# A GRU with an expert-choice layer: the two bias rows are loaded in runs of 32 numbers with gaps between them

## The reference, cut to what matters

```python
def cell(h, x):                       # 256 steps, one after the other
    gi = x @ W_ih + b_ih              # 512 -> 3 * 512
    gh = h @ W_hh + b_hh
    r, z = sigmoid(i_r + h_r), sigmoid(i_z + h_z)
    n = tanh(i_n + r * h_n)
    h_new = (1.0 - z) * n + z * h
...
S = softmax(hs @ router_w + router_b)          # 4096 tokens x 16 experts
G, idx = top_k(S.T, 256)
y[idx] += G * (hs[idx] @ expert_w + expert_b)
out = x + y
```

## Time and profile before

| what | value |
|---|---|
| median of 3 runs (lowest to highest) | 1097.17 us (1095.88 to 1097.18) |
| the profiled execution | 1096.32 us, span 1094.6 us |
| TensorE (PE) busy | 1081.6 us, 99% of the span |
| VectorE (DVE) busy | 857.2 us, 78% |
| ScalarE (ACT) busy | 411.3 us, 38% |
| chain that ended last | PE 96%, DVE 1%, DMA 1% |
| granted TensorE clock, mean | 0.998 |

### The profile page before, as it was taken

How to read it: one execution, slowest core, us unless ns; L and a number is a source line. 1 busy time by engine, 2 the same in 40 slices (tenths; PEclk the granted TensorE clock), 3 DMA queues, 4 the chain that set the end, 5 groups by cost and what they waited for, 6 DMA issues and landing times.

```text
span 1094.6 us, 60966 instructions
## 1 busy us (share of the span) xinstructions
PE 1081.6 (99%) x26752; PEld 892.5 (82%) x26752; DVE 857.2 (78%) x4601; ACT 411.3 (38%) x1658; POOL 15.5 (1%) x42
## 2 busy tenths in 40 slices
PE   7999999999999999999999999999999999999998
PEld 5788888888888888888888888888888888888852
DVE  5788777877777877787777778778788777777897
ACT  1333333434333434333333333333333333333561
POOL 5000000000000000000000000000000000000000
PEclk9999999999999999999999999999999999999999
DMA  7311000000000000000000000000000000000369
GB/s 255 90 22 23 13 13 13 6 11 13 13 13 13 14 13 6 11 13 13 14 13 14 13 5 12 13 13 13 13 13 12 6 12 14 3 3 4 100 175 308
DMA packets 80448, 36.78 MB, mean 34 GB/s; under 512 B 70052, under 2 KB 70308, under 8 KB 80183
## 3 DMA queue, kind: packets, MB, share of 16 engines
q1 hardware_dynamic: 77840, 28.79, 10.8%
q10 hardware_dynamic: 2342, 4.11, 1.2%
HBM read 24.49 MB, written 8.39 MB: 30 GB/s over the span
## 4 chain that ended last, share of the span: by engine, by line
PE 96%; DVE 1%; DMA 1%; SPq 0%; ACT 0%; issue 0%; DVEq 0%
PE gates L819 60%; PE gates L756 26%; PE ffn_ps L883 3%; PE gates L937 3%; DMA whh<-in_L_cond_W_hh 1%; PE gates L915 1%; PE ffn_ps L937 1%; PE log_ps L972 1%; PE gates L949 0%; DVE wih L1417 0%; SPq L376 0%; PE ffn_ps L915 0%; DVE u L1186 0%; SPq L379 0%; DVE wih L1507 0%
## 5 line engine op out<-in xcount | busy, mean ns | idle before, releaser
L819 PE MATMUL gates<-whh,tok 128*16 128x192 f32 x16384 | 713.9, 326 | 3.5 <-DVE tok L1211 1.9
L819 PEld LDWEIGHTS gates<-whh,tok 128*16 128x16 f32 x16384 | 562.5, 123 | 104.5 <-DVE tok L1211 3.3
L518 ACT ACTIVATE th<-gates 128x128 f32<-128x128 f32 x512 | 139.8, 273 | 341.7 <-PE gates L819 341.5
L1186 DVE SCALAR_TENSOR_TENSOR u<-th,gates 128x64 f32<-128x64 f32 x512 | 113.5, 222 | 167.0 <-ACT th L518 166.7
L523 ACT ACTIVATE n_t<-v 128x64 f32<-128x64 f32 x512 | 131.5, 257 | 277.9 <-DVE v L1190 277.9
L756 PE MATMUL gates<-wih,xS 128*32 128x192 f32 x3024 | 146.3, 326 | 0.0
L1202 DVE STREAM_TRANSPOSE nT<-n_t 128x64 f32<-128x64 f32 x512 | 123.7, 242 | 0.0
L1193 DVE STREAM_TRANSPOSE zT<-th 128x64 f32<-128x64 f32 x512 | 122.0, 238 | 0.0
L1190 DVE SCALAR_TENSOR_TENSOR v<-u,gates 128x64 f32<-128x64 f32 x512 | 113.1, 221 | 8.8
L756 PEld LDWEIGHTS gates<-wih,xS 128*32 128x32 f32 x3024 | 100.1, 110 | 21.0
L1211 DVE SCALAR_TENSOR_TENSOR tok<-new_n,z_h 128x32 f32<-128x32 f32 x512 | 110.1, 215 | 8.7
(11 more groups left out here) (202 smaller groups left out, 622.2 us busy)
## 6 DMA issues: line engine op xcount, KB each, us to landing
x_in<-in_x SPq DMA_DIRECT2D x248, 32.0 KB, 2.2
out<-tok SPq DMA_DIRECT2D x15, 256.0 KB, 4.7
xs<-in_x SPq DMA_DIRECT2D x14, 256.0 KB, 3.7
out<-tok ACTq DMA_DIRECT2D x14, 256.0 KB, 4.6
wih<-in_L_cond_W_ih SPq DMA_DIRECT2D x4, 768.0 KB, 7.1
whh<-in_L_cond_W_hh SPq DMA_DIRECT2D x4, 768.0 KB, 13.7
whh<-in_x SPq DMA_DIRECT2D x12, 256.0 KB, 3.6
we<-in_L_ffn_expert_w SPq DMA_DIRECT2D x4, 256.0 KB, 2.8
```

The source lines that it names most:

```text
L518: nc.scalar.activation(th[a][:, :, :].rearrange("p g c -> p (g c)"), gates[t // S % PAIRS][a][:, R_:HN], ACT.Tanh, scale=0.5).then_inc(th_ ...
L819: mm = nc.tensor.matmul(gates[t // S % PAIRS][a][Q * j:Q * j + rows, R_:GC].rearrange("b (g k c) -> b g k c", g=G, k=KH), columns, by_tile ...
L1186: V.scalar_tensor_tensor(u[a][:, :], th[a][:, 0, :], 1.0, ps[a][:, HN:GC], ALU.add, ALU.mult).then_inc(u_ready[a], 1)
```

## The change: what it does, and the diff

Before, each bias row was 1536 numbers side by side on one partition. Now each is 48 runs of 32 numbers, and a run begins 40 numbers after the one before it, so that 8 numbers stay unused between runs. The row takes 1920 columns in place of 1536, within four tiles. The three loads name the runs on both sides of the transfer: 16 runs, 32 runs and 48 runs of 128 bytes. The matmuls of line 1006 read the same 192 numbers each, in the same order, at other strides. Nothing else differs.

```diff
-        bih, bhh = (tok[0:1, PAD + n * D:PAD + (n + G) * D].rearrange("p (g c) -> p g c", g=G) for n in (NT - 8, NT - 12))
+
+        RUN, RUNS = 40, D // Q
+        bih, bhh = (tok[0:1, PAD + n * D:PAD + n * D + G * RUNS * RUN].rearrange("p (r c) -> p r c", c=RUN)[:, :, 0:Q]
+                    for n in (NT - 8, NT - 12))
...
-            act.dma_start(bih[:, 0, :], b_ih.rearrange("(o g c) -> o g c", o=1, g=G)[:, 2]).then_inc(b_loaded, 16)
-            act.dma_start(bih[:, 1:, :], b_ih.rearrange("(o g c) -> o g c", o=1, g=G)[:, 0:2]).then_inc(b_loaded, 16)
-            act.dma_start(bhh, b_hh.rearrange("(o g c) -> o g c", o=1, g=G)).then_inc(b_loaded, 16)
+            act.dma_start(bih[:, 0:RUNS, :], b_ih.rearrange("(o r c) -> o r c", o=1, c=Q)[:, 2 * RUNS:, :]).then_inc(b_loaded, 16)
+            act.dma_start(bih[:, RUNS:, :], b_ih.rearrange("(o r c) -> o r c", o=1, c=Q)[:, 0:2 * RUNS, :]).then_inc(b_loaded, 16)
+            act.dma_start(bhh, b_hh.rearrange("(o r c) -> o r c", o=1, c=Q)).then_inc(b_loaded, 16)
...
-                                              b[:, :, a * HC * J:(a + 1) * HC * J].rearrange("p g (k j c) -> p j g k c", j=J, c=Q)[:, j],
+                                              b.rearrange("p (g a k j) c -> p a j g k c", g=G, a=2, j=J)[:, a, j],
```

## The result

| kernel | median (lowest to highest), runs | ratio to before, 95% interval |
|---|---|---|
| before | 1096.16 us (1095.05 to 1097.18), 18 | |
| changed | 1098.28 us (1096.71 to 1100.03), 18 | 1.0019 [1.0013, 1.0025] |

The changed kernel is about 2.1 us slower. That is 0.19%, clear of zero; the interval of 0.13 to 0.25% reaches over the bound of 0.2% that the prediction set, so on which side of it the loss lies is not settled. The forecast was 1097.3 us and no change; the time lies in the range of 1095.6 to 1099.4.

A forecast was written before the change was run, and what follows sets the result against it. Matmuls bound the loop, and the last W_hh block's landing bounds the start. Packets +0.11 us, with issues, landing and matmul strides at 0, on a 1097.17 us median gave 1097.3 us, in effect no change; range 1095.6 to 1099.4.

The forecast's parts named there:

- What bounds the kernel: Whole kernel: matmuls bound the loop, TensorE holding 96% of the chain; the start waits for the last W_hh block.
- the number of packets: Queue q10 at the start: 144 packets for the bias loads in place of 6, 138 more, all before 7 us.
- the matmuls' strides: Bias matmuls of line 1006: same runs of 32 numbers at other strides, cost 0, bounds 0 to 0.8 us.
- Cover of 1.57 us: Step 0, waiting for W_hh: biases or `h0` may land up to 1.57 us later without moving the time.
- Issues on ScalarE: ScalarE at the start: `h0` issued up to 0.30 us later, hidden by the 1.57 us of cover, so 0.
- Landing of `h0`: Start: `h0` and biases land 0.4 us later (bounds 0.11 to 3.88), under the 1.57 us of cover, so 0.
- rival A: Queue turns: `h0` waits extra W_ih blocks, deciding after 8.4 us; +0.8 us (0.17), or +2.7 or half clock (0.07).
- the prediction's own signs: Step 0's last group: wrong if its W_hh wait is gone, or it starts after 22 or before 20.7 us.
- The clock: TensorE at the start: longer idling could hold half clock through 76 passes, +2.4 us less remaining cover; not in the sum.
- Packets on the engines: Transfer engines at the start: 9 small packets each delay the last W_hh block, +0.11 us, bounds -0.37 to +0.42.
- B: Relief at the start: last W_hh block lands 0.37 to at most 0.92 us earlier, 1096.3 to 1096.8 us; chance 0.09.
- C: Bias loads not shared: each stays on one engine, +0.7 us there, 1097.9 us if the straggler, otherwise 1097.2; chance 0.04.

The follow-up runs named there:

- h0_issue_mid: Kernel before, biases one packet each, with ScalarE waiting for GpSimd's fourth mask step before issuing `h0` (2.43 us); ratio 1.0015 to before.
- only_bhh: Changed kernel with `b_ih` laid out and loaded as before, only `b_hh` in 48 runs with gaps; ratio 1.0015 to before.
- late_fill: Kernel before with `h0` issued late (2.59 us) behind GpSimd's fifth mask step, plus 20 zero-writing matmuls in TensorE's idle time; ratio 1.0005 to before.
- fill_after: Changed kernel plus 20 zero-writing matmuls on TensorE just before its wait for `h0`; ratio 1.0011 to before.
- three_issues: Changed kernel with `b_ih` in one load of 48 runs instead of two, bias matmuls 24 instead of 16; ratio 1.0007 to before.
- three_fill: Changed kernel with `b_ih` in one load instead of two, plus 20 zero-writing matmuls in TensorE's idle time; ratio 1.0011 to before.
- h0_first: Changed kernel with the load of `h0` issued ahead of the three bias loads; ratio 1.0011 to before.
- h0_issue_late: Kernel before, biases one packet each, with ScalarE waiting for GpSimd's fifth mask step before issuing `h0` (2.58 us); ratio 1.0014 to before.

## Why the prediction was right, and which step of it failed

- **What bounds the kernel, the number of packets (138 more), the matmuls' strides (0):** right. (That all these packets would be through before 7 us was not: queue q10 had packets up to 7.8.)
- **Cover of 1.57 us:** the right kind of bound, a little small; the profiles give 1.99, since the 0.84 us of a group overlaps the next group.
- **Issues on ScalarE, up to 0.30 us later, costs nothing:** this term was mis-sized. The issues of loads spread over 16 engines take 0.60 to 0.65 us, not 0.22 to 0.52, and `h0` went out 0.67 us later. I took the largest issue among one-packet loads as the bound for spread ones. How little would have been allowed: 2.43 us is too late with nothing in front (h0_issue_mid), and 2.25 was too late behind one shared load (only_bhh).
- **Landing of `h0`, 0.4 us later:** this is the step that failed. I let the late issue pass on into the landing one to one, and let the small loads leave together. It was 1.50 us, because the landing is a step: before, `h0` moved by 6.2 us; issued at 2.43 us or later with nothing in front it moved from 6.0 us on, and in the changed kernel `b_hh` moved up to 6.2 us in its place. The forecast "`h0` by 7.3 us" is refuted; the rule "later than 8.4 us" at which rival A was to decide was just missed, 8.33, and the clock decided instead. By the prediction's own signs it is wrong: the wait before the last group is gone, and that group starts after 22 us, since step 0 begins at 21.41 and its matmuls end at 24.2.
- **The clock:** priced within rival A as a companion, and left out of the forecast. It was the larger half: 2.01 + 0.72 us against 1.50. The profiles of late_fill and fill_after show that with the `h0` and bias matmuls at full clock the late `h0` stays under the cover.
- **Packets on the engines, +0.11 us:** the last W_hh block can be read from SyncE's first `x_in` issue, which waits for it: 21.08 before, 21.23 in three_issues and 21.33 in three_fill, near the forecast, but 22.39 in the changed kernel and 21.96 in fill_after, beyond the bound of +0.42. In the changed kernel it is off the chain, because TensorE is later still; in fill_after it is the loss that is left. What adds that microsecond is open: it is not the small packets alone, since h0_first has them all and 21.16.
- **Rival A**, given 0.24 in all, had the right outcome (late `h0`, the wait for W_hh gone, half clock, +0.8 to +2.7 us), and its reason, a turn more behind W_ih, fits the packets: `b_hh` in the place of `h0`, `h0` in the next. What it lacked is that a late issue does the same without any load in front. The two are not told apart here.
- **B** is refuted by the chain, and nothing landed earlier. **C**, each load on one engine, would give 96 data packets and 3 marks in place of 6 packets, 93 more; the page has 138 more.

That the time fell into the range is in part luck. The range was drawn towards rival A, and its base was too high: the 3 runs of before had a median of 1097.17, the 18 have 1096.16. The forecast change was +0.11 us and the measured one +2.1, so 2.0 us of loss were missed, and the base hid half of it. From 1096.16 the same working gives 1096.3, and a range up to 1098.4, with 1098.28 just inside. The Trainium skill (DMA: Bandwidth & Descriptors, "Issuing engines are not separate DMA queues") calls the time to initiate a transfer usually small beside the transfer. The trace agrees, 0.60 us of issue against 5.52 us to the landing of `h0`; but the 0.67 us by which it was issued later are more than this start had room for.

## What to carry to other kernels

A small load that must get in between big ones has a place to catch, so count the issues in front of it, with the duration that a load over that many engines really has, and look for the last issue time that still makes it. See also in the packets by stretch of time whether another load of the same queue now moves in its place. Cover measured in microseconds is cover at the clock of that profile: where a wait ahead of a dependent chain of matmuls grows, price the chain once more at half clock before calling it hidden.

## What the runs showed of the hardware that was not expected

- The time to issue depends on how the load is cut: 0.22 to 0.52 us for one-packet loads, 0.60 to 0.65 us for 16, 32 or 48 runs over 16 engines, and 1.45, 0.66 and 0.74 us for 4, 8 and 12 runs. It depends on what was issued before as well: the same load of `h0` took 0.34 to 0.41 us first or behind one-packet loads and 0.52 to 0.60 behind spread ones.
- The landing of a small load on the second queue, beside a full first queue, went in a step with its issue time: its matmuls started at 6.83 to 7.00 for issues at 2.08 to 2.16 us, and at 8.28 to 8.48 for 2.25 to 2.77. In the changed kernel each spread load had a stretch of its own in queue q10: 32 packets by 2.8 us, 48 from 3.0 to 4.0, 61 from 5.4 to 6.2 and 35 from 6.2 to 8.0.
- 20 matmuls that write zeros into idle time put off the half clock until the projection and shortened it: of 11 runs 7 fell to a mean of 0.996 or less without them (h0_issue_late) and none with them (late_fill).
